# A vision-transformer tower on one Trainium2 core: mixer and experts worked by half of a pair's tokens

## The reference, cut to what matters

```python
h = tok(x, ...)              # 32 x 32 queries per image; for each, 8 heads sample 8 points
                             # bilinearly, project them to keys and values, softmax over points
h = concat(cls, h)           # 1 + 1024 tokens of 64 channels
h = h + attn(layernorm(h))   # RWKV mixer: k, v, r; a scan over the tokens; Wo; then an FFN 64-256-64
h = h + ffn(layernorm(h))    # router: argmax over 32 experts; expert MLP 64-16-64
```

## Time and profile before

| what | value |
|---|---|
| median of 3 runs | 2805.5 us |
| the profiled execution, own time | 2803.6 us |
| its span (first to last instruction) | 2801.7 us |
| mean granted TensorE clock | 0.952 |
| busy: PE, DVE, ACT, POOL | 85%, 85%, 48%, 71% |
| HBM traffic | 305.62 MB read, 8.40 MB written, 112 GB/s |

### The profile page before, as it was taken

The page is one execution under the profiler, slowest core; times in us unless marked ns, Lnnn a source line. Parts: engine busy times, 40 slices in busy tenths (PEclk is TensorE's granted clock), DMA queues, the critical chain, the costliest instruction groups (busy, mean ns, idle before and its releaser), DMA issues. The chain is left out here.

```text
span 2801.7 us, 34581 instructions
## 1 busy us (share of the span) xinstructions
PE 2391.6 (85%) x10646; PEld 1561.1 (56%) x10680; DVE 2385.7 (85%) x3808; ACT 1350.2 (48%) x2326; POOL 1983.2 (71%) x2052
## 2 busy tenths in 40 slices
PE   4588889888988888898888889888888988889887
PEld 4455555655655555655555556555556556555533
DVE  5889989889998989998898989888998988888741
ACT  2345444544544444464444446444444645444563
POOL 4777777777777777777777777777777777777400
PEclk7799999999999999999999999999999999999999
DMA  4333333434343343434334343433434343333200
GB/s 161 118 119 117 119 119 103 126 118 127 118 126 118 105 123 116 127 117 127 118 111 128 108 126 118 125 118 113 127 106 126 118 125 119 111 104 103 72 0 15
DMA packets 139228, 314.70 MB, mean 112 GB/s; under 512 B 68912, under 2 KB 69296, under 8 KB 134960
## 3 DMA queue, kind: packets, MB, share of 16 engines
q0 software_dynamic: 98304, 268.57, 32.7%
q1 hardware_dynamic: 40880, 45.58, 4.8%
HBM read 305.62 MB, written 8.40 MB: 112 GB/s over the span
## 5 line engine op out<-in xcount | busy, mean ns | idle before, releaser
L471 POOL DMA_INDIRECT gathered<-pixels,index x2048 | 1983.0, 968 | 649.2 <-issue 614.8
L527 PE MATMUL points_ps<-c_sb,weighed 128*128 128x128 f32 x4096 | 542.4, 290 | 230.8 <-DVE weighed L1063 230.3
L1063 DVE TENSOR_TENSOR weighed<-gathered,tables 128x1024 f32<-128x1024 f32 x512 | 600.4, 1214 | 125.8 <-DMA gathered<-pixels,index 123.9
L527 PEld LDWEIGHTS points_ps<-c_sb,weighed 128*128 128x128 f32 x4096 | 494.9, 150 | 339.7 <-DVE weighed L1063 286.4
L539 PE MATMUL kv_ps<-kv_sb,sampled_t 128*128 128x256 f32 x2048 | 473.4, 385 | 26.6 <-DVE products L1091 26.4
L721 ACT ACTIVATE sampled_t<-points_ps 128x512 f32<-128x512 f32 x256 | 153.1, 598 | 710.1 <-PE points_ps L527 710.1
L539 PEld LDWEIGHTS kv_ps<-kv_sb,sampled_t 128*128 128x128 f32 x2048 | 388.0, 192 | 112.6 <-DVE products L1091 41.2
L617 PE MATMUL work_ps<-nm,w_sb 128*128 128x512 f32 x544 | 291.6, 619 | 38.0 <-DVE xm L1253 35.3
L486 PE MATMUL work_ps<-hn,w_sb 128*128 128x512 f32 x544 | 267.4, 616 | 12.9 <-DVE hn L1115 10.2
L849 ACT ACTIVATE moe_hidden<-work_ps,v_sb 128x512 f32<-128x512 f32 x272 | 186.7, 687 | 161.5 <-PE work_ps L618 144.2
L1098 DVE TENSOR_REDUCE scores<-products 128x128 f32<-128x1024 f32 x128 | 246.0, 1922 | 0.0
(11 more groups left out here) (169 smaller groups left out, 3124.4 us busy)
## 6 DMA issues: line engine op xcount, KB each, us to landing
grid_px<-grid SPq DMA_DIRECT2D x32, 1024.0 KB, 5.6
gathered<-pixels,index POOLq DMA_INDIRECT x2048, 2.7
out<-rm SPq DMA_DIRECT2D x32, 256.0 KB
w_sb<-weights SPq DMA_DIRECT2D x1, 1984.0 KB, 8.9
moe_hidden<-consts SPq DMA_DIRECT2D x1, 512.0 KB, 9.8
attended<-cls SPq DMA_DIRECT2D x1, 512.0 KB, 11.5
c_sb<-consts SPq DMA_DIRECT2D x1, 192.0 KB, 5.2
w_sb<-weights SPq DMA_DIRECT2D x1, 192.0 KB, 5.1
```

The source lines that it names most:

```text
L471: pool.indirect_dma_start(gathered[:, n % RING, k * PATCH:(k + 1) * PATCH], None, pixels, bass.IndirectOffsetOnAxis(ap=index[:, n // TILES ...
L527: mm = pe.matmul(points_ps[:, j * P:(j + 1) * P], weighed[:, n % 2, at:at + 2 * C], ident, is_transpose=True, start=(q == 0), stop=(q == 3))
L1063: ins = dve.tensor_tensor(to[:, :, :, e, :], g[:, :, e, :, :], wt[:, :, e, :].unsqueeze(3).broadcast_to([P, HEADS // 2, 4, C]), ALU.mult)
```

## The change

- The sampling order of a pair: the first 8 tiles are now the first half of the tokens of both images, the last 8 the second half. `attended`, the grid loads, the corner weights, the sampling points and the index bases follow this.
- The mixer and the experts work on half a pair (512 columns) at a time. The scan goes through in 2 pieces of 256 per half, as it went in 4 per pair. Activations on 1024 columns become two on 512. `choose` works on half the tokens.
- A half's mixer starts 4 slots after its sampling ends and takes slots 4 to 29 counted from there; its experts take slots 33 to 51. The same order therefore repeats every 16 slots, once for each half. `m0` and `m1` are the mixer of the two halves, `e0` and `e1` the experts.
- The class token goes through as a second half alone.
- The tables for the last iterations are gone: the same order holds to the end. The first three iterations are unrolled instead of two.
- SP loads the grid in two transfers of 512 KB per half, and stores each half in two transfers.

```diff
-PIECES = 4
-PIECE = NQ // PIECES
+PIECES = 2
+PIECE = HALF // PIECES
...
+IN_AT = 4
+TEMPLATE = [
+    (48, "e", ["md"]),
+    (33, "e", ["cenm"]),
+    (34, "e", ["varm"]),
+    (3, "q", ["qt0", "qt1"]), (51, "e", ["out"]),
+    (20, "m", ["wo"]), (IN_AT, "m", ["in"]), (4, "m", ["cena"]), (4, "q", ["qo0", "qo1"]),
+    (5, "m", ["vara"]), (21, "m", ["cenf"]),
+    (22, "m", ["varf"]), (38, "e", ["route"]),
+    (24, "m", ["gate"]),
+    (9, "m", ["k", "v", "r"]), (25, "m", ["up.0", "up.1"]),
+    (26, "m", ["up.2", "up.3"]), (42, "e", ["one"]),
+    (43, "e", ["mu.0", "mu.1"]),
+    (28, "m", ["dn"]), (44, "e", ["mu.2", "mu.3"]),
+    (45, "e", ["mu.4", "mu.5"]),
+    (14, "q", ["ht"]), (14, "q", ["of"]), (46, "e", ["mu.6", "mu.7"]),
 ]
+FIRST_LOOPED = 3
+def place(kind, h, after):
+    at = after - 16 * (1 - h)
+    return f"{kind}{h}{at // 32:+d}", at % 32
...
+QUERY_AT = {"grid_corners": 2, "features": 7, "normalised": 9, "gelu": 12, "sampling_points": 15}
+MIXER_AT = {"mix_input": 8, "running_max": 12, "running_sums": 14, "mixed_sums": 16, "mixed_exponent": 18, "mixed": 20,
+            "add_mix": 21, "ffn_input": 24, "gate_exponent": 26, "add_ffn": 29}
+EXPERT_AT = {"moe_input": 37, "take_logits": 39, "choose": 42, "add_moe": 51}
+SCALAR_QUERY_AT = {"feature_std": 8, "gelu_exp": 10}
+SCALAR_AT = {"update": 12, "output": 13, "mixed_log": 16, "mixed_quotient": 18, "gate": 27}
...
-LAST_SCHEDULE = [
...
-            pe.wait_ge(attended_ready.sem, attended_ready.at(it - 1, TILES // 2 + 2 * h + 2))
+            pe.wait_ge(attended_ready.sem, attended_ready.at(run - 1, TILES // 2 * (h + 1)))
...
-                sp.dma_start(grid_px[:, :, :].rearrange("p t n -> p (t n)"),
-                             grid[2 * (it + 1) + b, :, :]).then_inc(grid_loaded.sem, 16)
+                of = slice(b * TILES // 2 * PATCH, (b + 1) * TILES // 2 * PATCH)
+                for i in range(2):
+                    sp.dma_start(grid_px[:, i * TILES // 2:(i + 1) * TILES // 2, :].rearrange("p t n -> p (t n)"),
+                                 grid[2 * (it + 1) + i, :, of]).then_inc(grid_loaded.sem, 16)
...
-                n = mark(act.activation(wide[:, 2, :], hn[:, :], ACT.Relu, bias=decay[:, 3:4]))
+                n = mark(act.activation(wide[:, 2, cols(h)], hn[:, cols(h)], ACT.Relu, bias=decay[:, 3:4]))
...
-                dve.tensor_scalar(index[:, b, :], corner[:, :, 0], image_base[:, 0:1], None,
-                                  ALU.add).then_inc(index_ready.sem, 1)
+                for of in range(2):
+                    at = slice(of * TILES // 2 * HEADS, (of + 1) * TILES // 2 * HEADS)
+                    last = dve.tensor_scalar(index[:, b, at], corner[:, at, 0], image_base[:, of:of + 1], None, ALU.add)
+                last.then_inc(index_ready.sem, 1)
...
-                dve.tensor_tensor(attended[:, t:t + 2, b, :].rearrange("p t (h d) -> p t h d", h=HEADS),
+                of, at = t // (TILES // 2), TILES // 2 * b + t % (TILES // 2)
+                dve.tensor_tensor(attended[:, at:at + 2, of, :].rearrange("p t (h d) -> p t h d", h=HEADS),
```

More of the change, by code:

```diff
@@ L57 @@
 T_GRID = 4 * TILES * HEADS
-T_DECAY = T_GRID + 4 * TILES
+T_DECAY = T_GRID + 2 * 4 * TILES
 SLOTS = 4 * (2 * TILES) // 2
-SCHEDULE = [
[11 rows of a table removed]
-]
[L80 to L86, removed]
@@ new lines, with schedule @@
+FIRST_LOOPED = 3
+def place(kind, h, after):
+    at = after - 16 * (1 - h)
+    return f"{kind}{h}{at // 32:+d}", at % 32
+def schedule():
+    rows = []
+    for n, (after, kind, names) in enumerate(TEMPLATE):
+        for h in range(2):
+            part, slot = (f"q{h}", after + 16 * h) if kind == "q" else place(kind, h, after)
+            rows.append((slot, n, part, names))
+    return [(slot, part, names) for slot, _, part, names in sorted(rows, key=lambda row: row[0:2])]
+SCHEDULE = schedule()
@@ L97, with work_uses @@
 QUERIES_AT = (17, 1)
-LAST_SCHEDULE = [
[8 rows of a table removed]
[L108 to L116, removed]
 ROUND = float(2 ** 23)
 GELU_CUBE = 0.044715
-def work_uses(schedule, parts):
-    names = [(part, name) for _, part, group in schedule if part in parts for name in group]
+def work_uses(parts):
+    names = [(part, name) for _, part, group in SCHEDULE if part in parts for name in group]
     return {key: n for n, key in enumerate(names)}, len(names)
@@ L159, in vit_kernel @@
     pairs = images // 2
[L160 to L166, removed]
+    first_looped, last_looped = FIRST_LOOPED, pairs - 2
+    all_parts = tuple(sorted({part for _, part, _ in SCHEDULE}))
+    names_of = {part: [name for _, of, group in SCHEDULE if of == part for name in group] for part in all_parts}
     def parts_of(it):
@@ L435, in iteration @@
             def iteration(it):
                 parts = parts_of(it)
-                for b in range(2):
+                stores = [(slot // 16, part) for slot, part, names in SCHEDULE if names == ["out"] and part in parts]
+                for h in range(2):
                     if "q0" in parts:
-                        load_grid(it, b)
-                if 2 in parts:
-                    store(it)
+                        load_grid(it, h)
+                    for when, part in stores:
+                        if when == h:
+                            store(it, part)
@@ new lines, in running_sums, with mixed_sums @@
+                after(p)
+            def mixed_sums(it, part):
+                run, h = run_of(it, part), half_of(part)
+                pieces = [piece(h, c) for c in range(PIECES)]
+                dve.wait_ge(output_gates.sem, output_gates.at(run, h))
+                for at in pieces:
+                    a = mark(dve.tensor_tensor(hn[:, at], wide[:, 0, at], state_q[:, at], ALU.mult))
+                for at in pieces:
+                    mark(dve.tensor_tensor(rs1[:, at], wide[:, 1, at], rs1[:, at], ALU.mult))
+                for at in pieces:
+                    b = mark(dve.tensor_tensor(wide[:, 0, at], wide[:, 0, at], state_p[:, at], ALU.mult))
@@ L1186, in mixed @@
+            def mixed(it, part):
+                run, h = run_of(it, part), half_of(part)
+                dve.wait_ge(quotient.sem, quotient.at(run, h))
+                for at in (piece(h, c) for c in range(PIECES)):
+                    last = dve.tensor_tensor(wide[:, 0, at], wide[:, 0, at], hn[:, at], ALU.mult)
                 last.then_inc(mixed_ready.sem, 1)
-                if isinstance(it, int) and it == 0:
+                if isinstance(run, int) and run == 0:
                     for state in (state_o, state_p, state_q):
-                        step(dve.tensor_copy(state[:, 0:1], state[:, 1:2]))
@@ L1203, in gate_exponent, with add_mix @@
-            def gate_exponent(it):
-                dve.wait_ge(gate_log.sem, gate_log.at(it, 2))
-                for c in range(PIECES):
-                    last = dve.tensor_tensor(rs2[:, piece(c)], rs2[:, piece(c)], relu_r[:, piece(c)], ALU.add)
+                        step(dve.tensor_copy(state[:, 0:1], state[:, HALF + 1:HALF + 2]))
+            def add_mix(it, part):
+                h = half_of(part)
+                bank, done = full(dve, it, part, "wo")
+                dve.tensor_tensor(x1[:, cols(h)], x1[:, cols(h)], bank, ALU.add).then_inc(done, 1)
@@ new lines, in iteration @@
+                    for name, stage in (("mix_input", mix_input), ("running_max", running_max),
+                                        ("running_sums", running_sums), ("mixed_sums", mixed_sums),
+                                        ("mixed_exponent", mixed_exponent), ("mixed", mixed), ("add_mix", add_mix)):
+                        for part in parts_at(it, j, "m", MIXER_AT[name]):
+                            stage(it, part)
+                    for name, stage in (("moe_input", moe_input), ("take_logits", take_logits), ("choose", choose),
+                                        ("add_moe", add_moe)):
+                        for part in parts_at(it, j, "e", EXPERT_AT[name]):
+                            stage(it, part)
```

751 lines of the change are left out of this document (363 added, 388 removed), and 19 rows, old and new, of tables (LAST_SCHEDULE, SCHEDULE).

## The result

The changed kernel took 3008.9 us (median of 4 runs, 3004.8 to 3045.7) against 2805.2 us beside it: 1.0754 times the time before, with an interval of 1.071 to 1.0799. The direction was forecast, the size was not: +204 us where +55 stood, 9 us past the upper end of the range. The profiled execution took 3004.77 us and spans 3002.9.

A forecast was written before the change was run, and what follows sets the result against it. The prediction held that POOL's gathers set the pace, 81.5 us a half. With halves of 84.2 us, 27 x 2.7 = 73 us were added and 18 taken off the tail: 2803.6 + 73 - 18 = 2858.6, say 2861 us; range 2780 to 3000.

The forecast's parts named there:

- What bounds and the counts: POOL's gathers set the pace, 81.5 us a half; finer cutting adds an estimated 0.6 us per half on DVE.
- the front: Before the first gather: one more transfer and one more small copy, below 1 us, taken as 0.
- DVE's 74.8 us a half: DVE's time per half: 73.0 us busy, plus 0.6 for finer cutting, plus 1.2 for dependent steps.
- the 6.7 us of slack: What DVE may wait per half on PE and ACT before POOL, at 81.5 us, has to wait for DVE.
- The loop through `md`, `varm` and `add_moe`: `varm` needs the bank `md` filled, read by `add_moe` behind `attend`; PE stops some 4 us, DVE waits 8.4 a half.
- The chain behind `add_moe`: From `add_moe` through `varm` to the exponentials that `attend` needs: 18.1 us, beside 9.7 us of DVE work.
- the fast side: Rival: POOL keeps the pace, DVE's waits stay within its 6.7 us, only the tail counts; 2787.5 us, chance 0.26.
- Other waits, "1 us": All waits of a half outside the loop through `md`, `varm` and `add_moe`: taken as 1 us.
- The period: Time of a steady half: 74.8 + 8.4 + 1 = 84.2 us, 2.7 over POOL's 81.5, for 27 full halves.
- The rule weighed against the trace: The Trainium skill's rule: a wait recurring every loop round lets PE's clock fall each round; one 3.19 us wait agreed.
- the second rival: Lower clock behind PE's stops at `varm` and `mu7`, 3 us a half for one: 2942 us, both 3030; chance 0.27.
- The tail, -18 us: Behind the last gather: 16.5 us less PE work, divided by busy share 0.79 gives 21; taken as 18, bounds 0 and 45.

The follow-up runs named there:

- run 3: Both edits on the changed kernel: `add_moe` one slot earlier on DVE, the exponentials one slot earlier on ACT; 2792.1 us, 0.9953.
- Runs 1 to 3: On the changed kernel: `add_moe` one slot earlier on DVE, 2856.4 us; exponentials one slot earlier on ACT, 2897.8 us; both edits, 2792.1 us.
- run 4: Changed kernel plus five products of 512 columns that nobody reads, on PE ahead of `varm`; 2961.8 us, 1.0555.
- Run 5: Kernel with both edits plus one unread PE product behind each of 30 groups of fills in the last two iterations; 2791.1 us, 0.9945.

## Why the prediction was right or wrong

*What bounds and the counts: right; the front: near.* DVE's busy time is 2390.0 us against 2385.7, so the finer cut cost 4 us over 32 halves, 0.1 a half, where 0.6 was allowed. The first gather starts at 28.8 us, 2.7 later than in the earlier trace rows, where I took below 1. The grid's transfers were waited for once, ahead of the first gather (5.0 us where 3.4 stood), the stores not at all.

*DVE's 74.8 us a half and the 6.7 us of slack: right in kind.* In the steady stretch DVE is busy 146.08 of 176 us, 73.6 of 88.64. When the waits were cut in run 3 it kept POOL's pace, as the slack says.

*The loop through `md`, `varm` and `add_moe`: found where it was placed, but it was not one loop.* PE stops once a half for `xm`'s reader (144.7 us in 30), 4.55 us where "some 4" stood. The chain behind `add_moe`, costed at 18.1 us, measures 21.25 - 0.68 (the step `add_moe` itself) = 20.6; with PE kept busy it is 18.6. So the sum of rows was 0.5 us short, and the other 2.0 us are the lower clock. DVE waits 11.1 us in it, not 8.4. I treated the wait as one whose end is the chain's end; that holds for its length, but hid that two causes make it. Runs 1 to 3 show two, in series: 5.6 us behind `varm`, and 5.5 us behind ACT's order from `in` to the exponentials, which stays although `varm` no longer waits. The chance that I gave to the fast side rested on one stop being removed; it would have needed two.

*Other waits, "1 us": too low.* The period of 88.64 us less 73.6 busy less 10.9 in the stretch (20.6 less 9.7 of work) leaves 4.1 us for waits elsewhere and the steps between instructions, where 1 + 1.2 stood. The largest wait among them is `feat_b`'s for ACT, 53.1 us in 31, 1.7 a half.

*The period:* 84.2 forecast, 88.64 measured. Of the 4.4 us too little, 2.0 are the clock, 0.5 the rows of the chain and the remaining 2 the other waits. 28 x 4.4 = 123 us, and the 28th half, which I had not counted as full, is 3 more; with the tail's 12 (below) that is 138 of the 148 us by which the forecast was short. The step that failed is this sum: the chain was costed at full clock throughout, with the lower clock left outside as a rival (18.1 us where 20.6 came), and the other waits were put at 1 us with no row behind it (with the steps 2.2 where 4.1 came). That the halves' waits would exceed DVE's slack was right; their size was not.

*The rule weighed against the trace.* Behind a stop of 4.55 us the granted clock of the next 10.9 us is 0.77, between the lower level of 1.2 GHz and full speed, and `varm` took 2.08 us. The mean of its 66 instructions is 1084 ns where run 4 has 640, so it happened in nearly every half. The Trainium skill (TensorE: Matmul & The Clock Gate, HAM oscillation) tells of a matmul loop whose wait for a DMA recurs, and that the clock falls in every round of it; at this place, where the wait is for DVE, the trace agrees. Behind the stop of 2.00 us at `mu.7` the clock is 1.00 and the projection 3.62 us, and so in all 26 halves from 300 to 2600 us: there the changed kernel lost no clock, though run 4 did behind the same stop in 12 of 26. So the second rival was half right: one place of two, at 2.0 us and not 3, and on top of a wait that was longer than the forecast had it. Its 2942 us for one place is 2860 + 27 x 3; the same sum with 2.0 is 2914, and the rest up to 3005 is the other waits and the chain's rows (28 x 2.5 = 70), the smaller gain in the tail (12), the 28th half and the start.

*The tail, -18 us: the working failed.* PE's work behind the last attended tile fell from 118.07 to 104.69 us: 13.4 less, near the 16.5 counted. But the stretch fell from 148.9 to 143.0 only, 5.9 us, because I divided by PE's busy share as if PE were the length of the tail. Run 5 shows that it isn't: 26 us of work more, 1.0 us longer. With both edits the tail is 135.6 us, 13.3 less than before; so 7.4 us of the missing 12 went with the same two edits, and the clock rose with them (0.87 to 0.92); how the 7.4 divide between the waits and the clock isn't shown.

*The signs named beforehand.* Gathers waiting for `weighed` by 50 us or more: 205.1. The last gather some 60 us later: 175.8. DVE's wait for gathers nearly gone: 23.4. `products` waiting some 5 us a half for `probs`: 175.3 / 32 = 5.5. PE waiting for `xm`'s reader: yes. Two signs were badly chosen. "The granted clock well under 0.95" did not come (0.96 in the steady stretch where 0.94 stood, and 0.96 in both kernels from 300 to 2600 us), although the clock did cost 2 us a half: a mean over a pair hides a short fall at the one place where it counts. And "170 us or more" behind the last gather came (195.4), for another reason: POOL, no longer the pace, runs ahead of DVE by its ring, and the last attended tile ends 52 us behind the last gather where it was 21. The tail has to be measured from the last attended tile.

## What to carry to other kernels

When a cut into finer units puts producers and consumers closer together, write down for each bank or buffer who reads it last, and where that reader stands in its own engine's list; two readers a slot too late cost 7% here, and moving each by one slot turned the loss into a small gain of 0.5%. Waits in series are not one wait: ask of each whether it stays when the one before it is gone. And where no engine is busy all the time, work taken from the busiest one need not come off the time: in the tail 13.4 us less of it on PE went with 5.9 us.

## What the hardware showed that was not expected

Products that nobody reads made the kernel faster: 148.4 us of additional PE work, laid into a stop of 4.55 us, took 47 us off the time, because the 0.3 us wait that remained left the following products at 1.12 and 3.62 us instead of 2.08 and 5.11. In the tail of the kernel with both edits the same means raised the granted clock from 0.92 to 0.99 and gained nothing (2791.1 against 2792.1 us, within their intervals); that the added products held up as much as the clock gave back fits this, but isn't shown.

The clock's mean says little about which order is faster. The rows of the stretch from 300 to 2600 us, of the kernel before, the changed kernel and the kernel with both edits:

```profile
300.00:2600.00 2300.00, 2022.59 (x9193) 1334.09 (x9220) 2059.29 (x3240) 1129.28 (x1953) 1749.40 (x1808) 0.96 0.40 118
```

```profile
300.00:2600.00 2300.00, 1883.20 (x8488) 1230.09 (x8487) 1912.50 (x3076) 1042.17 (x1950) 1621.61 (x1677) 0.96 0.38 110
```

```profile
300.00:2600.00 2300.00, 2012.94 (x9229) 1306.97 (x9228) 2081.59 (x3328) 1138.46 (x2113) 1747.70 (x1814) 0.97 0.41 119
```

The clock is 0.96, 0.96 and 0.97, at periods of 81.5, 88.6 and 81.2 us a half. A shorter stretch can mislead: from 1000 to 1176 us the kernel with both edits has 1.00 and the kernel before 0.94, and over the long stretch that difference is nearly gone.
